# Two graph layers on one core: first layer written without loops, one addition for sums and statistics, a third round of row slots, half-size end rounds, and a middle stage in units of four blocks

## What is computed

```
h = relu(layernorm(x))                                     x: 6250 x 128
x = x + attention(h, src, dst)      4 heads of 32 channels, 106250 edges sorted by dst, then one own loop a node:
      z = h W + b;  logit = leaky_relu(z . alpha);  softmax over the edges of a dst;  sum of weight * z[src];  + bias
h = relu(layernorm(x))
x = x + (h + segment_sum(msg, dst))
      ef  = (relu(edge_attr We1 + be1) We2 + be2) * sigmoid(edge_weight Wt + bt)
      msg = relu([h[src], ef] Wn1 + bn1) Wn2 + bn2
```

## Time and profile before

| | |
|---|---|
| median of 3 runs | 2428.14 us (2425.41 to 2434.88) |
| the profiled execution | 2425.41 us, its span 2423.5 us |
| busy: PE, DVE, ACT, POOL | 67%, 66%, 36%, 69% |
| granted PE clock, mean | 0.726 |
| stage A, to the first gather | 0 to 60.96 us |
| stage B, gathers of the first layer | 60.96 to 1168.9 us |
| stage B, after the last gather | 1168.9 to 1237.7 us |
| stage C, to the second layer's first gather | 1237.7 to 1344.8 us |
| stages D and E | 1344.8 to 2423.5 us |

### The profile page before, as it was taken

How to read it: one execution, slowest core, us unless ns; L and a number is a source line. 1 busy time by engine, 2 the same in 40 slices (tenths; PEclk the granted TensorE clock), 3 DMA queues, 4 the chain that set the end, 5 groups by cost and what they waited for, 6 DMA issues and landing times. The chain is left out here.

```text
span 2423.5 us, 38425 instructions
## 1 busy us (share of the span) xinstructions
PE 1618.7 (67%) x8526; PEld 1120.6 (46%) x8526; DVE 1592.1 (66%) x5419; ACT 869.4 (36%) x2652; POOL 1666.3 (69%) x1705
## 2 busy tenths in 40 slices
PE   4136555455454555545564789888888998888897
PEld 3024434344343343434463455555555555555555
DVE  4257777676776777767757666666666666666665
ACT  5123332423324233242316333333343343333331
POOL 3777776676676676677216677777777777777774
PEclk9555565556555655566556798998998889889988
DMA  4222222222222222222000544444444444444443
GB/s 133 49 55 56 54 53 50 53 50 50 50 53 50 49 53 49 50 53 50 18 3 31 146 139 137 130 131 130 131 130 131 130 131 130 130 131 130 131 130 84
DMA packets 95384, 208.59 MB, mean 86 GB/s; under 512 B 30273, under 2 KB 58271, under 8 KB 85280
## 3 DMA queue, kind: packets, MB, share of 16 engines
q0 software_dynamic: 53248, 110.01, 18.5%
q1 hardware_dynamic: 41584, 97.35, 14.2%
q10 hardware_dynamic: 432, 0.13, 0.0%
HBM read 197.70 MB, written 9.67 MB: 86 GB/s over the span
## 5 line engine op out<-in xcount | busy, mean ns | idle before, releaser
L408 POOL DMA_INDIRECT rows<-table,index x832 | 797.4, 958 | 325.7 <-issue 236.2
L982 POOL DMA_INDIRECT rows<-table,index x832 | 798.2, 959 | 262.3 <-issue 249.0
L623 PE MATMUL bank<-onehot,rows 128*128 128x128 f32 x1664 | 403.3, 418 | 29.9 <-ACT rows L688 29.9
L501 DVE TENSOR_SCALAR onehot<-iota_row,dst_rel 128x128 f32<-128x128 f32 x832 | 258.2, 311 | 219.0 <-PE bank L623 134.8
L623 PEld LDWEIGHTS bank<-onehot,rows 128*128 128x128 f32 x1664 | 346.7, 309 | 115.1 <-ACT rows L688 70.4
L688 ACT ACTIVATE rows<-rows,edge_w 128x32 f32<-128x32 f32 x1664 | 360.4, 308 | 0.8
L1058 ACT ACTIVATE msg<-pre 128x512 f32<-128x512 f32 x208 | 130.9, 630 | 592.1 <-DVE pre L1091 592.1
L1103 DVE TENSOR_TENSOR acc<-acc,bank 128x128 f32 x832 | 238.9, 287 | 148.2 <-issue 36.5
L1032 PE MATMUL bank<-onehot,msg 128*128 128x128 f32 x1664 | 246.0, 295 | 119.8 <-ACT msg L1058 119.7
L1023 PEld LDWEIGHTS bank<-wn1b,ef 128*128 128x128 f32 x1664 | 241.1, 209 | 124.5 <-issue 108.5
L1032 PEld LDWEIGHTS bank<-onehot,msg 128*128 128x128 f32 x1664 | 222.4, 208 | 130.1 <-issue 62.7
(11 more groups left out here) (154 smaller groups left out, 1273.7 us busy)
## 6 DMA issues: line engine op xcount, KB each, us to landing
ts<-in_ts SPq DMA_DIRECT2D x52, 1024.0 KB
rows<-table,index POOLq DMA_INDIRECT x1664, 2.5
ea<-in_ea_t SPq DMA_DIRECT2D x52, 512.0 KB, 5.7
table<-feat SPq DMA_DIRECT2D x7, 455.0 KB, 4.1
x_rows<-in_x SPq DMA_DIRECT2D x7, 448.0 KB, 6.6
table<-proj SPq DMA_DIRECT2D x7, 448.0 KB, 3.0
out<-x_rows SPq DMA_DIRECT2D x6, 448.0 KB, 3.2
dn<-in_dst_halo SPq DMA_DIRECT2D x26, 33.5 KB
```

The costliest lines, as they stand in the source:

```text
L408: gp.indirect_dma_start(rows0[:, i % 2, k * TG + t, :], None, table1, bass.IndirectOffsetOnAxis(index[:, n:n + 1], 0)).then_inc(gathered[i ...
L501: dve.tensor_scalar(onehot[:, k % 2, t, :], iota_row[:, :], dst_rel[:, ds(i * RT + k * TG + t, 1)], None, ALU.is_equal).then_inc(oh0, 1)
L623: last = pe.matmul(bank[k % 2][:, t * P:(t + 1) * P], rows0[:, q, k * TG + t, 0:CH], onehot[:, k % 2, t, :], start=True, stop=True)
L982: gp.indirect_dma_start(rows[:, k, t, :], None, table2, bass.IndirectOffsetOnAxis(index[:, n:n + 1], 0)).then_inc(gathered[2][k], 16)
```

## The change

- **Loops.** Stage B is written out, round by round. The numbers of tiles and columns in masks and waits are constants; the columns in `acc` still come from registers.
- **One addition.** `acc` and `acc_w` are the two halves of `acc2`; PE writes a group's sums and its statistics into two neighbouring banks (`pair0` or `pair1`), the statistics of tile t at columns t*128, and one addition a tile over [128, 2, 128] replaces L508 and L512. Elsewhere the bank of statistics holds zeros, set once.
- **Row slots.** `rows0` has 24 groups (`RING`); the gather of group g waits for the sums of group g-24. Landing is counted by halves of a round.
- **Rounds.** 27 rounds: four groups, 25 times eight, four groups. In each round the maxima of the next are worked out at its end: `scan_rows` after the third last group, `scan_row_ends` after the second last, `full_maxima` after the last; PE turns the weights before it spreads the deltas; ACT scales all groups of a round, then takes up the next round's logits.
- **Middle stage.** 13 units of four blocks (the last has one). PE turns `acc_w` block by block and DVE sums the four tiles' parts (a reduction over [128, 4, 5, 4]); the shares are taken in two parts, after three units and after the rest; mean and variance come from `bn_stats` and `bn_aggr`, one of each a block, in place of two reductions, a scaling and ACT's squares; `proj` holds all blocks, and SP no longer waits for each write.

Stages A, D and E compute as before.

```diff
+UB = 4
+UNITS = -(-NB // UB)
+EARLY = 3
 TG = 4
...
+RING = 3 * RG
+SPAN_SIZES = [HALF] + [RG] * (ROUNDS - 1) + [HALF]
+SPANS = [(sum(SPAN_SIZES[:r]), z) for r, z in enumerate(SPAN_SIZES)]
+TURNS = len(SPANS)
+assert sum(SPAN_SIZES) == GROUPS and all(z % HALF == 0 for z in SPAN_SIZES)
 
...
-        bank = [ctx.enter_context(nc.psum_tensor(f"bank{n}", [P, 512], fp32)) for n in range(8)]
+        pair = [ctx.enter_context(nc.psum_tensor(f"pair{n}", [P, 2, 512], fp32)) for n in range(2)]
+        upper = [ctx.enter_context(nc.psum_tensor(f"bank{n}", [P, 512], fp32)) for n in range(4, 8)]
+        bank = [pair[n // 2][:, n % 2, :] for n in range(4)] + [b[:, :] for b in upper]
+        both_sums = [pair[n][:, :, :] for n in range(2)]
+        row_sums = [bank[0], bank[2]]
+        stat_sums = [bank[1], bank[3]]
...
-        acc = sb("acc", [P, ACCW])
-        acc_w = sb("acc_w", [P, ACCW])
-        stat_pick = sb("stat_pick", [P, LCOL])
+        acc2 = sb("acc2", [P, 2, ACCW])
+        acc = acc2[:, 0, :]
+        acc_w = acc2[:, 1, :]
...
-                    for i in range(ROUNDS):
-                        for k in range(RG):
-                            if i >= 2:
-                                gp.wait_ge(agg0, RG * (i - 2) + k + 1)
-                            for t in range(TG):
-                                n = i * RT + k * TG + t
-                                gp.indirect_dma_start(rows0[:, i % 2, k * TG + t, :], None, table1,
-                                                      bass.IndirectOffsetOnAxis(index[:, n:n + 1], 0)).then_inc(gathered[i % 2][k], 16)
+                    for g in range(GROUPS):
+                        if g >= RING:
+                            gp.wait_ge(agg0, g - RING + 1)
+                        for t in range(TG):
+                            n = g * TG + t
+                            gp.indirect_dma_start(rows0[:, g % RING, t, :], None, table1,
+                                                  bass.IndirectOffsetOnAxis(index[:, n:n + 1], 0)).then_inc(half_in[g % RING // HALF], 16)
...
-                    def mask(i, k, t):
-                        dve.tensor_scalar(onehot[:, k % 2, t, :], iota_row[:, :], dst_rel[:, ds(i * RT + k * TG + t, 1)], None,
-                                          ALU.is_equal).then_inc(oh0, 1)
-
-                    def add(i, k, t, v, first):
-                        fresh = first and k == 0
-                        if not (fresh and t == 0):
-                            dve.wait_ge(acc0, (i * RG + k) * TG + t)
-                        dve.tensor_tensor(acc[:, ds(v, P)], acc[:, ds(v, P)], bank[k % 2][:, t * P:(t + 1) * P], ALU.add).then_inc(acc0, 1)
-                        if not fresh:
-                            dve.wait_ge(accw0, (i * RG + k) * TG + t - TG + 1)
-                        of = slice(t * Q4, t * Q4 + LCOL)
-                        dve.tensor_tensor(acc_w[of, ds(v, P)], acc_w[of, ds(v, P)], bank[2 + k % 2][of, 0:P], ALU.add).then_inc(accw0, 1)
+                    def mask(n):
+                        dve.tensor_scalar(onehot[:, n // TG % 2, n % TG, :], iota_row[:, :], dst_rel[:, n:n + 1], None, ALU.is_equal).then_inc(oh0, 1)
+
+                    def add(n, v):
+                        if n:
+                            dve.wait_ge(acc0, n)
+                        dve.tensor_tensor(acc2[:, :, ds(v, P)], acc2[:, :, ds(v, P)], both_sums[n // TG % 2][:, :, n % TG * P:(n % TG + 1) * P],
+                                          ALU.add).then_inc(acc0, 1)
...
+                    def sum_group(g, at):
+                        dve.wait_ge(agg0, g + 1)
                         for t in range(TG):
-                            if k + 2 < RG:
-                                mask(i, k + 2, t)
-                            elif not last:
-                                mask(i + 1, k + 2 - RG, t)
-                            add(i, k, t, at[k % HALF * TG + t], first)
-
+                            if g + 2 < GROUPS:
+                                mask((g + 2) * TG + t)
+                            add(g * TG + t, at[t])
...
+                    for r in range(1, TURNS + 1):
+                        span = groups(r - 1)
+                        for k, g in enumerate(span):
+                            if k and k % HALF == 0:
+                                at = first_of(g)
+                            sum_group(g, at[k % HALF * TG:(k % HALF + 1) * TG])
+                            if r == TURNS:
+                                continue
                             if k == 0:
-                                penalties(i, q, n)
+                                penalties(r)
                             if k == 1:
-                                keep_row_penalties(i)
-                            if last:
-                                continue
-                            if k == 2:
-                                scan_rows(i)
-                            if k == 4:
-                                scan_row_ends(i)
-                            if k == 5:
-                                full_maxima(i)
...
+                                keep_row_penalties(r)
+                            if g == span[-3]:
+                                scan_rows(r)
+                            if g == span[-2]:
+                                scan_row_ends(r)
+                            if g == span[-1]:
+                                full_maxima(r)
+                        dve.wait_ge(acc0, (span[-1] + 1) * TG)
+                        if r < TURNS:
+                            at = first_of(groups(r)[0])
+                            rescale(r, at)
...
                         for t in range(TG):
-                            pe.matmul(bank[2 + k % 2][t * Q4:t * Q4 + LCOL, 0:P], edge_w[:, q, k * TG + t, :], onehot[:, k % 2, t, :], start=True, stop=True)
+                            pe.matmul(stat_sums[g % 2][t * Q4:t * Q4 + LCOL, t * P:(t + 1) * P], edge_w[:, r % 2, k * TG + t, :], onehot[:, g % 2, t, :],
+                                      start=True, stop=True)
...
-                            if k == 6:
-                                spread_delta(i)
-                                turn_weights(i)
...
+                    for r in range(1, TURNS + 1):
+                        span = groups(r - 1)
+                        for k, g in enumerate(span):
+                            sum_group(r - 1, g)
+                            if r == TURNS:
+                                continue
+                            if k == 0:
+                                turn_penalties(r)
+                            if g == span[-3]:
+                                turn_logits(r)
+                            if g == span[-2]:
+                                turn_row_ends(r)
+                            if g == span[-1]:
+                                turn_carries(r)
+                        if r < TURNS:
+                            turn_weights(r)
+                            spread_delta(r)
...
+                    for r in range(TURNS):
+                        keep_logits(r)
+                        exponentials(r)
+                        keep_weights(r)
+                        factors(r)
+                        act.wait_ge(ew_ready, 2 * (r + 1))
+                        for g in groups(r):
+                            scale_group(r, g)
...
+                    for u in range(UNITS):
+                        own_term(u)
+                    for u in range(UNITS - EARLY):
+                        keep_features(u)
+                    gp.wait_ge(s_t, UNITS)
                     gp.memset(acc[:, :], 0.0).then_inc(cleared, 1)
...
+                    def turn_stats(u):
+                        if u >= 2:
+                            pe.wait_ge(sums_kept, u - 1)
+                        for j, b in enumerate(each(u)):
+                            last = pe.transpose(bank[6 + u % 2][:, j * P:(j + 1) * P], acc_w[:, b * P:(b + 1) * P], ident[:, :])
+                        last.then_inc(sw_t, 1)
...
+                    def gather_stats(u):
+                        dve.wait_ge(sw_t, u + 1)
+                        dve.tensor_reduce(sums_t[:, blocks(u), 0:LCOL], psum_rows(bank[6 + u % 2], u).rearrange("p b (t c) -> p b c t", t=TG)[:, :, 0:LCOL, :],
+                                          AX.X, ALU.add).then_inc(sums_kept, 1)
...
+                    def scaled_sums(u):
+                        if u == 0:
+                            dve.wait_ge(ca_ready, 2)
+                        dve.wait_ge(s_t, u + 1)
+                        if u >= 2:
+                            dve.wait_ge(mixed, u - 1)
+                        dve.tensor_tensor(heads(part[:, u % 2, 0:upto(u + 1) - upto(u)]), heads(psum_rows(bank[u % 2], u)), per_head(sum_scale, u),
+                                          ALU.mult).then_inc(parted, 1)
+
+                    def mix(u):
+                        dve.wait_ge(parted, u + 1)
+                        dve.wait_ge(own, u + 1)
```

(27 more changed lines are left out.)

688 lines of the change are left out of this document (303 added, 385 removed).

## The result

| | before | after |
|---|---|---|
| median of 4 runs | 2427.71 us (2425.41 to 2434.88) | 2305.18 us (2304.47 to 2306.63) |
| ratio, 95% interval | | 0.9491 (0.9471 to 0.9512) |
| span of the profiled execution | 2423.5 us | 2303.4 us |
| stage B, first gather to last addition | 60.96 to 1237.7 | 61.65 to 1149.8 |
| stage C, to the next layer's first gather | 107.1 | 73.7 |

122.5 us faster; forecast were 100 (2328 us, 2308 to 2370). The direction and both places were right, and the time lies 3 us under the range. Against the forecast span of 2324.2 us the measured 2303.4 is 20.8 us shorter, made up of: first gather +0.7, all gathers -1.9, what follows the last gather -8.0 (40.0 for 48), stage C -12.8, stages D and E +1.2.

The account below looks back on a forecast made before the run. Stage B was held by DVE's 43.35 us round over the gathers' 40.1. Stage B's end at 1159 (-79), stage C 86.5 (-20.5) and an unchanged 1078.7 gave a 2324 span; plus 4.6, 2328 us, range 2308 to 2370.

Parts of the forecast that it names:

- A group becomes 4 x (0.31 + 0.42 + 0.01) = 2.95 us.: Stage B on DVE: four masks and four joined additions take 2.95 us instead of 3.44, saving 3.9 a round.
- rival 1: Stage B: the joined addition takes 0.58 us, DVE still bounds, total 2377 (2350 with 0.54); chance 0.09.
- 7.8 us go, since those steps leave the middle of the round.: Stage B round on DVE: idle times of 2.43, 2.80, 1.89 and 0.67 us vanish as the maxima move to its end.
- short waits: Stage B round's serial end: some 0.5 us added within the 7.0 us charged for that piece.
- the half round saves time at the end: Stage B's end: last half round's gathers take 20.2 us, round 25's end at 1091, so the stage ends at 1159.
- With slots for three rounds they wait for no slot: Stage B gathers on POOL: they become the bound at 40.1 us a round and never wait for a row slot.
- 1.75 us a round on the mean: Stage B loops on DVE: the back branch costs 3.5 us in every second round, none after the change.
- about these 10: Stage C: POOL's work on x delays DVE operations reading two tensors; about 10 us of this was kept.
- rival 2: Stage C: POOL delays each small statistic by 0.68 us, total 2361 (half of them) to 2395 (all); chance 0.07.
- The last units' drain: Stage C's end: 3 us charged after the main part, before write and barrier.
- Rivals 3 and 4: Stage B: stalls remain, last gather 1168.9, total 2386, chance 0.03; serial round end costs 8 us more, time 2453, chance 0.05.
- -32: Stage C: the largest gain with `bn` operations at their bounds, -32 to -7 us, around the forecast -20.5.

Follow-up runs that it names:

- equal rounds: Changed kernel with 26 equal rounds in place of a half round at each end: 2308.8 us for 2431.3 in the kernel before.
- POOL quiet: Changed kernel with POOL's three middle-stage operations cut to one column in each block: 2298.2 us for 2434.7; 2939.5 us when rows landed slowly.
- the last maxima alone: Changed kernel with 26 equal rounds and the last round's maxima behind all groups of the round before: first 2932.2 us for 2997.3, again 2302.8 us.
- The same in the kernel before: Kernel before with each tile's statistics in columns of their own, added over all 128 partitions instead of five: 2346.3 us for 2428.2 (0.9665).

## Why the prediction was right and wrong

- *What bounds.* Right: stage B was held by DVE's round, and gathers took over at 40.1 us a round. Last gather forecast 1111, measured 1109.8.
- *"A group becomes 4 x (0.31 + 0.42 + 0.01) = 2.95 us."* This step failed. The addition was right at 0.42 (rival 1, at 0.54 to 0.58, is out), but I added durations, as the rows of before allowed, where starts were 0.31 apart. That spacing belonged to the pieces at partitions 32 to 96 that the change removes. Measured 2.20: 8 x 0.75 = 6.0 us a round less.
- *"7.8 us go, since those steps leave the middle of the round."* This failed too, the other way. The 2.43 us among them are not a step of the maxima that moved, but PE's stand for the penalties behind the first group, which the change keeps; 2.18 of them are still there (the row at 1114.37). In the kernel before, just ahead of the mask at 486.48:

```profile
483.40 0.38 PE L577 MATMUL bank<-ident,row_pen 66*1 66x66 f32 x2 [11.81 <-DVE row_pen L452]
```

- *The round.* 37 less 6.0 plus 2.2 is 33.2; measured 32.4; I had added 0.5 for short waits, and the rest is not told apart. The runs give the same sum in other parts: from 41.6 writing out the loops takes 1.1 (forecast nothing), the rewritten round adds 2.1 (forecast 0.8 less), the joined addition takes 10.2 (forecast 3.9).
- *The end of B.* First addition of round 25 forecast 1110.5, measured 1108.5; then 32.4 for 37 and 8.9 for 11.3 (the last groups at 2.2 to 2.3). Sum -9. The gathers' end, 58 of the 79 us forecast for stage B, was right by its mechanism. That the half round saves time at the end, as I read my sum, is wrong: with equal rounds B ends within 2 us.
- *Third slots, loops.* "With slots for three rounds they wait for no slot" holds for two as well. The loops I priced at one row, 1.75 us a round on the mean; alone they are worth 61 us in the kernel before, and beside the joined addition they are part of the some 5 us that four edits share.
- *Stage C.* POOL's contention was right in size and kind: "about these 10" for 9.8 measured (71.6 - 61.8), and `bn_stats` free of it (rival 2 is out). Of the 12.8 us 1.4 lie ahead of the first scaled sums and 0.7 in the write and the barrier. The other 10.7 are the same fault as in B: where no input is waited for, operations of 512 at 0.69 start 0.57 to 0.60 apart, eight short ones fit into 1.07 us where I had 1.5, and with POOL quiet a unit takes 3.12 us for 4.2, 13 us in all. The last units' drain, from the last statistics to the last bias, gives 2.6 back (5.6 for 3).
- *Rivals 3 and 4.* The stalls went. The serial end of a round cost the 6.6 us of the earlier trace rows, and the rewritten round 2.9 more than I counted, far from the 8 more that would have made the kernel slower.
- *The range.* Its lower end took in stage C's bounds but nothing for the group in B's round, whose spacing I took as fixed. Either error alone, 9 us in B or 12.8 in C, would have left the time inside; together they put it 3 us below. The bounds were loose besides: eight short operations at my lower 0.155 are 3 us less for the stage than my sum, not the 11.5 that "-32" stands for.

## What to carry to other kernels

On DVE price a row of operations from start to start, and ask what holds the starts apart before removing an operation: a slice of five partitions at an offset cost more here than 128 partitions from 0 (0.84 us a tile for 0.59). Before an idle time is taken off, name the instruction that it waits for and see whether the edit moves that one. When an edit moves a stage under another engine's pace, further edits there are worth next to nothing: compare the counted round with the pace of the gathers first. At the end of a stage count the chain of rounds on each engine, not only the distance from the last transfer.

## What the runs showed of the hardware

- Start positions on DVE: 0.20 us from start to start for 128x128 operations that all begin at partition 0, 0.30 to 0.32 for a piece at partition 32, 64 or 96 and for the mask and the addition behind it, with durations of mostly 0.27 to 0.29 either way.
- A 128x256 addition of 0.42 us was followed after 0.33, one of 128x512 of 0.69 us after 0.57 to 0.60, where the next did not wait for its result.
- At one time the same gathers landed more slowly. In the first run with the last maxima alone POOL's row is:

```profile
L424 POOL DMA_INDIRECT rows<-table,index x832 | 795.9, 957 | 523.1 <-issue 223.4 <-PE pair L641 149.4 <-remote 135.6
```

  Issuing one took the same 0.957 us, but 32 took 51 us instead of 40, and the kernel before 2997 us instead of 2430. The three variants of the changed kernel that ran then were 2% under it, where such are 5% under it elsewhere. DVE's and POOL's work in stage C took its usual time. What slowed the landing was not tried. It need not be the chip: the run "The same in the kernel before" has the same chip number, 26 minutes later, and there the kernel before took its usual 2428 us.
